# Sums of weights and of operands moved from GpSimd to VectorE, and splits, takes and casts reordered around them, in a two-layer kernel with seven-product blocks

## The reference

```python
# layer 0: grouped convolution along the row, context and bias, then a dense layer with a low-rank part
out = conv(x, weight, groups=4, taps=9) + (cond @ c_weight.T)[:, :, None] + bias[None, :, None]
y   = out @ W.T + b                                   # 1024 -> 1024, on 2048 rows
probs = softmax(out @ gate_w.T + gate_b)              # 4 ranks: 8, 16, 32, 64
r   = the rank with the largest probability
x   = x + y + out @ A[:r].T @ B[:, :r].T

# layer 1: channels mixed by eight kernels weighted per sample, then a dense layer with 8 experts of rank 16
agg = einsum('bk,koi->boi', softmax(mlp(cond)), weight)
out = einsum('boi,bih->boh', agg, x) + agg_b[:, :, None]
w   = sparsemax(out @ W_router.T + b_router)
x   = x + out @ W_base.T + b_base + sum_e w_e (out @ A_e) @ B_e
```

## Time and profile before

| | us |
|---|---|
| median of 3 executions (525.5 to 528.06) | 525.73 |
| the profiled execution | 524.66 |
| its span, first to last instruction | 522.9 |
| TensorE busy with matmuls | 510.3 (98%) |
| VectorE busy | 349.2 (67%) |
| GpSimd busy | 166.5 (32%) |
| ScalarE busy | 129.2 (25%) |

### The profile page before, as it was taken

One profiled execution on the slowest core, in us unless ns is written; L12 is line 12 of the kernel. 1 busy time (PEld: TensorE's weight loads), 2 busy tenths in 40 slices (PEclk: granted clock), 3 DMA queues, 4 the chain that ended last, 5 costly groups with the idle time before them and its releaser, 6 DMA issues.

```text
span 522.9 us, 8726 instructions
## 1 busy us (share of the span) xinstructions
PE 510.3 (98%) x3237; PEld 481.5 (92%) x3237; DVE 349.2 (67%) x743; ACT 129.2 (25%) x270; POOL 166.5 (32%) x142
## 2 busy tenths in 40 slices
PE   8999999989999999999999979999999999999997
PEld 7899999989999999999998869999999999999986
DVE  1865598757666775767787488494867756585752
ACT  3721233313322222331252221111212111111200
POOL 1000771404434042432103353260616235070620
PEclk8999999999999999999999989999999999999999
DMA  8825304427476573656899943332514233340212
GB/s 288 325 76 178 132 2 135 133 67 222 143 249 204 189 261 122 233 159 229 263 418 310 411 149 105 104 123 81 181 52 167 84 116 107 109 155 18 100 46 80
DMA packets 41383, 85.32 MB, mean 163 GB/s; under 512 B 3931, under 2 KB 25435, under 8 KB 41340
## 3 DMA queue, kind: packets, MB, share of 16 engines
q1 hardware_dynamic: 31884, 61.38, 34.8%
q10 hardware_dynamic: 9456, 23.38, 12.3%
HBM read 59.30 MB, written 25.44 MB: 162 GB/s over the span
## 4 chain that ended last, share of the span: by engine, by line
PE 81%; DVE 8%; DMA 7%; issue 2%; SPq 1%; ACT 1%; POOL 0%; DVEq 0%; ACTq 0%
PE b_x L1154 6%; PE b_x L1156 6%; PE b_x L1157 6%; PE b_m L1103 5%; DMA x_scratch<-xs 4%; PE b_p L1138 4%; PE b_y L1154 4%; PE b_p L1140 4%; PE b_p L1139 4%; PE b_y L1157 4%; PE b_y L1156 4%; PE b_m L1115 2%; DMA xs<-x_scratch 2%; PE b_w L1156 2%; PE b_w L1154 2%
## 5 line engine op out<-in xcount | busy, mean ns | idle before, releaser
L489 POOL TENSOR_TENSOR xs<-xs,filt 128x464 f32<-128x464 f32 (+1 forms) x32 | 44.3, 1391 | 127.7 <-DMA xs<-x_scratch 127.6
L542 ACT CAST a_hi<-mixed 128x512 fp32r<-128x512 f32 x64 | 38.7, 619 | 167.5 <-DVE mixed L807 93.7
L819 DVE TENSOR_TENSOR s_lo<-mixed,s_hi 128x512 fp32r<-128x512 f32 x56 | 65.9, 1193 | 18.6 <-ACT s_hi L554 16.3
L1138 PE MATMUL b_p<-wp_hi,a_hi 128*128 128x232 f32 (+1 forms) x224 | 61.5, 275 | 0.5 <-DVE xs L910 0.5
L1139 PE MATMUL b_p<-wp_lo,a_hi 128*128 128x232 f32 (+1 forms) x224 | 61.5, 275 | 0.0
L1140 PE MATMUL b_p<-wp_hi,a_lo 128*128 128x232 f32 (+1 forms) x224 | 61.4, 274 | 0.0
L900 DVE TENSOR_TENSOR xs<-b_x,xs 128x464 f32<-128x464 f32 (+1 forms) x58 | 36.1, 622 | 33.4 <-PE b_x L1157 25.5
L462 POOL TENSOR_TENSOR mixed<-mixed 128x512 f32<-128x512 f32 x14 | 18.1, 1294 | 114.6 <-DVE a_lo L812 97.2
L554 ACT CAST s_hi<-mixed 128x512 fp32r<-128x512 f32 x56 | 34.8, 622 | 75.7 <-POOL mixed L462 35.7
L812 DVE TENSOR_TENSOR a_lo<-mixed,a_hi 128x512 fp32r<-128x512 f32 x64 | 45.2, 728 | 11.2 <-ACT a_hi L542 10.5
L1154 PE MATMUL b_x<-wb_hi,s_hi 128*128 128x464 f32 (+1 forms) x112 | 43.7, 390 | 3.0 <-DVE xs L900 3.0
(11 more groups left out here) (229 smaller groups left out, 1218.9 us busy)
## 6 DMA issues: line engine op xcount, KB each, us to landing
blk<-in_xblk SPq DMA_DIRECT2D x16, 516.0 KB, 3.7
blk<-x_scratch SPq DMA_DIRECT2D x16, 512.0 KB, 3.8
xs<-in_x SPq DMA_DIRECT2D x16, 296.0 KB, 4.7
x_scratch<-xs SPq DMA_DIRECT2D x16, 296.0 KB, 3.5
xs<-x_scratch SPq DMA_DIRECT2D x16, 280.0 KB, 3.2
out_dram<-xs SPq DMA_DIRECT2D x16, 280.0 KB, 2.5
w_raw<-in_wcat SPq DMA_DIRECT2D x8, 546.0 KB, 8.1
praw<-in_wcat ACTq DMA_DIRECT2D x8, 464.0 KB, 4.3
```

Source lines behind the costliest of these rows:

```text
L489: pool.tensor_tensor(xs[s][:, a:b], xs[s][:, a:b], bbase[:, a:b], ALU.add).then_inc(x_biased[q], 1)
L542: act.copy(a_hi[:, op, :, :], mixed[:, op, :, :]).then_inc(ahi_done[op], 1)
L819: dve.tensor_tensor(s_lo[:, i, :, :], mixed[:, S_AT[i], :, :], hi(s_hi[:, i, :, :]), ALU.subtract).then_inc(slo_done[i], 1)
L1138: pe.matmul(dst, x_hi, wp_hi[:, k, 0:PLAIN[l]], start=(k == 0), stop=False)
```

## The change

GpSimd loses the 16 subtractions of the sums of weights and the four operations of `sums(2)`; both become VectorE's (`t_sums(kc)` and `first_sums()`). ScalarE's and VectorE's lists are reordered around them: `split_ut(2)` and `gate_exp(3)` stand at other places, the splits of T3 come before `finish(0, 1)`, released by a new semaphore `b12_read` (after step k = 3 of tile 3) instead of by the end of tile 3. `finish(1, 1)` is taken apart: `take_plain` and the take of `b_z` come ahead of the splits of A21 and A22, the take of `b_w` behind `first_sums()`. In pair 2 VectorE's splits of S1 to S4 come ahead of the first take, and `split_ut(4)` comes behind `sum_mix(6, 0)`; ScalarE's four casts of S come ahead of `gate_exp(4)`. TensorE's and SyncE's lists keep their order; TensorE only signals `b12_read` in addition. The semaphores of the T sums exist for four slots instead of seven.

```diff
@@ GpSimd
-            pool.wait_ge(wlo_done, 2 * NCH)
-            pool.wait_ge(alo_done[A22], 2)
-            for kc in range(HK):
-                pool.tensor_tensor(raw_block(kc, 0), raw_block(kc, 1), raw_block(kc, 0), ALU.subtract).then_inc(t_sum, 1)
...
-            pool.wait_ge(gated, 4 * (2 * FULL + 2))
-            sums(FULL)
@@ ScalarE
             gate_exp(2)
-            split_ut(2)
             for kc in (2, 3):
                 for i in (T1, T2, T4):
                     split_t(i, kc)
-            gate_exp(3)
-            act.wait_ge(dense0_done, 4)
+            split_ut(2)
+            act.wait_ge(b12_read, 1)
             for kc in range(HK):
                 split_t(T3, kc)
+            gate_exp(3)
...
             split_a(A22, 2)
+            for i in S_ORDER:
+                split_s(i, FULL)
@@ VectorE
+            def t_sums(kc):
+                dve.tensor_tensor(raw_block(kc, 0), raw_block(kc, 1), raw_block(kc, 0), ALU.subtract).then_inc(t_sum, 1)
+                dve.tensor_tensor(raw_block(kc, 1), raw_block(kc, 3), raw_block(kc, 1), ALU.subtract).then_inc(t_sum, 1)
+                dve.wait_ge(t_sum, 4 * kc + 1)
+                dve.tensor_tensor(raw_block(kc, 3), raw_block(kc, 3), raw_block(kc, 0), ALU.subtract).then_inc(t_sum, 1)
+                dve.wait_ge(t_sum, 4 * kc + 3)
+                dve.tensor_tensor(raw_block(kc, 2), raw_block(kc, 2), raw_block(kc, 3), ALU.subtract).then_inc(t_sum, 1)
+            def first_sums():
+                dve.tensor_tensor(mixed[:, A22, :, :], mixed[:, A21, :, :], mixed[:, A22, :, :], ALU.add).then_inc(s_sum, 1)
+                dve.tensor_tensor(mixed[:, A21, :, :], mixed[:, A11, :, :], mixed[:, A21, :, :], ALU.subtract).then_inc(s_sum, 1)
+                dve.wait_ge(s_sum, 1)
+                dve.tensor_tensor(mixed[:, A11, :, :], mixed[:, A22, :, :], mixed[:, A11, :, :], ALU.subtract).then_inc(s_sum, 1)
+                dve.wait_ge(s_sum, 3)
+                dve.tensor_tensor(mixed[:, A12, :, :], mixed[:, A12, :, :], mixed[:, A11, :, :], ALU.subtract).then_inc(s_sum, 1)
...
             finish(1, 0)
+            t_sums(0)
+            t_sums(1)
             for i in (T1, T2, T4):
                 split_t(i, 0)
-            gate0(2)
+            t_sums(2)
             for i in (T1, T2, T4):
                 split_t(i, 1)
-            split_ut(2)
+            gate0(2)
+            t_sums(3)
             for kc in (2, 3):
                 for i in (T1, T2, T4):
                     split_t(i, kc)
+            split_ut(2)
+            for kc in range(HK):
+                split_t(T3, kc)
             finish(0, 1)
             gate0(3)
...
             sum_mix(5, 1)
+            take_plain(1, 1)
+            finish_first(1, 1)
             split_a(A21, 2)
             split_a(A22, 2)
-            finish(1, 1)
-            for kc in range(HK):
-                split_t(T3, kc)
+            first_sums()
+            finish_second(1, 1)
...
                 gate(2 * g + 1)
+                if g == FULL:
+                    for i in S_ORDER:
+                        split_s(i, g)
                 if g == PAIRS:
                     split_slot(B21, 1)
                 else:
                     take_first(g)
-                if g == FULL:
-                    split_ut(2 * g)
-                    for i in S_ORDER:
-                        split_s(i, g)
                 if g < LAST:
                     sum_mix(2 * g + 2, 0)
-                if g > FULL:
-                    split_ut(2 * g)
+                split_ut(2 * g)
@@ TensorE, in dense0
+                if T == 2 * FULL - 1 and k == HK - 1:
+                    ins.then_inc(b12_read, 1)
```

More of the change, by code:

```diff
@@ L188, in build @@
         t_sum = sem("t_sum")
-        thi_done = [sem(f"thi_done{i}") for i in range(SLOTS)]
-        tlo_done = [sem(f"tlo_done{i}") for i in range(SLOTS)]
+        thi_done = {i: sem(f"thi_done{i}") for i in SUMS_AT}
+        tlo_done = {i: sem(f"tlo_done{i}") for i in SUMS_AT}
         lbhi_done, lblo_done, bias_split = sem("lbhi_done"), sem("lblo_done"), sem("bias_split")
@@ L204, in build @@
         mix_done, sum_done = sem("mix_done"), sem("sum_done")
-        dense0_done = sem("dense0_done")
+        dense0_done, b12_read = sem("dense0_done"), sem("b12_read")
         pl_done = sem("pl_done")
@@ L967, in _, with finish_first, finish_second, finish @@
             split_ut(0)
-            def finish(s, g):
+            def finish_first(s, g):
                 dve.wait_ge((c11_done, c21_done)[s], g + 1)
                 take((b_x, b_z)[s], 2 * s, g, (fin11, fin21)[s])
+            def finish_second(s, g):
                 dve.wait_ge((c12_done, c22_done)[s], g + 1)
                 take((b_y, b_w)[s], 2 * s + 1, g, (fin12, fin22)[s])
+            def finish(s, g):
+                finish_first(s, g)
+                finish_second(s, g)
                 take_plain(s, g)
```

## The result

| | us | executions |
|---|---|---|
| before, beside the changed kernel | 525.5 (522.83 to 528.06) | 9 |
| the changed kernel | 520.91 (518.71 to 524.89) | 9 |
| ratio | 0.9935, 95% interval 0.9908 to 0.9961 | |
| profiled execution, its span, its clock | 520.59, 518.9, 0.999 | 1 |

The forecast was 523.6, in a range of 522.5 to 525.5: the direction was right, the size was not. The two other batches in which the changed kernel ran gave 0.9946 (0.9922 to 0.9971) and 0.9944 (0.9918 to 0.997), and medians of 523.0 and 522.64, so 520.91 is also a lucky median.

What follows compares the result with a forecast made beforehand. TensorE, busy for 510.3 of 522.9 us, was taken as the bound. Losing waits of 0.48 and 1.57 us takes the profiled 524.66 to 522.6, or 523.7 against the median, stated as 523.6; range 522.5 to 525.5.

Steps and rivals of the forecast that it cites:

- The two waits: TensorE's waits at `plain(5)`, 0.48 us, and at P5 of pair 2, 1.57 us, both forecast to go.
- VectorE's prices: VectorE's new list: 2.2 us per group of weight sums, 2.56 for tile 2's gate, 2.4 for four rests of S.
- Its cover: Margin by which `split_ut(4)` ends before TensorE wants it at `turn_u(5)`: 101.5 against 102.2, so 0.7 us.
- some tenths that TensorE needs to get going: Slow first matmul after a TensorE wait, 0.43 instead of 0.36 us; forecast set at 523.6, not 523.7.
- P5 can follow at 104.85: In pair 2, P4's last matmul starts at 104.5 and P5 follows without a wait: 1.57 us gone.
- what TensorE wants: At `rank0(2)`, TensorE was said to want `split_ut(2)` at 74.91; forecast to end at 74.3.
- faster by over 0.5%: Outcome under 523.1 us for the whole kernel: the second rival and about a fifth of the forecast's cases, chance 0.24.
- The second rival: More than the two waits: part of the 3.0 us layer-turn wait goes or restarts cost more; 522.7 to 523.1, chance 0.12.
- the likeliest case: The forecast itself for the whole kernel, both waits gone: 523.6 us, own range 523.0 to 524.4, chance 0.63.
- The dependent sums and the rule: VectorE's 16 weight sums: 8.8 us forecast, against 9.6 if each cost its full 0.60 by the skill's rule.

Runs made afterwards that it cites:

- experiment 3: Changed kernel with `take_plain` back behind the splits of A21 and A22 and `first_sums()` behind `finish(1, 1)`'s last part: 522.59 us, 0.995 to the kernel before.
- experiment 4: Changed kernel with `split_ut(4)` moved one step back, behind `sum_mix(6, 1)`: 523.97 us, 0.9975 to the kernel before.
- experiment 6: Changed kernel with the four sums of operands of pair 2 back on GpSimd, behind its memset: 524.48 us, 0.9984 to the kernel before.
- experiment 5: Changed kernel with the 16 sums of weights back on GpSimd, other steps in the changed order: 526.32 us, 1.0017 to the kernel before.
- experiment 7: Changed kernel with 24 unneeded additions on GpSimd beside VectorE's sums of weights: 531.48 us in one execution.
- experiment 10: Changed kernel with the first 432 columns of two of four `xs` regions for pair 8 loaded earlier: 523.86 us, 0.9959 to the kernel before.

## Why the prediction missed, step by step

**What held.** The two waits went, both and fully. VectorE's prices came out as worked out: 2.19 to 2.20 us per group of sums (2.2 forecast), 2.57 for the gate (2.56), 2.48 for the rests of S (2.4), 2.54 for the four sums of operands (2.5). From there the whole list was right to some tenths, in its own time (the start is 1.11 later, by `turn_u(2)`): T3's rests, the takes, `gate0(3)` waiting for TensorE's `b_p`. `split_ut(4)` ended at 102.60 - 1.11 = 101.49, where 101.5 was forecast. Its cover was 0.34 us instead of 0.7 because TensorE came at 102.94 - 1.11 = 101.83 and not at 102.2: the mistake of the next paragraph, seen from the other side.

**The term that was mis-sized** is the worth of the two waits: "So the change can give back at most about 0.48 + 1.57 = 2.05 us". That took the bracket for the price. The bracket counts from the end of the last matmul's row, but in a full pipeline the next one starts long before that end: rows of 0.36 us start 0.20 apart. By starts, from these rows of the kernel before and those of the earlier trace rows:

```profile
74.69 0.35 PE L1227 MATMUL b_w<-wb_hi,a_lo 128*128 128x432 f32 x1
75.21 0.36 PE L1184 MATMUL b_x<-lb_lo,ut_lo 97*128 97x432 f32 x1
...
89.89 0.27 PE L1140 MATMUL b_p<-wp_hi,a_lo 128*128 128x228 f32 x1
90.86 0.28 PE L1139 MATMUL b_p<-wp_lo,a_hi 128*128 128x228 f32 x1
...
107.17 0.36 PE L1156 MATMUL b_y<-wb_lo,s_hi 128*128 128x432 f32 x1
```

| | last start to first start | ordinary pitch | next pitch, ordinary | worth | bracket |
|---|---|---|---|---|---|
| `plain(5)` | 90.65 - 89.89 = 0.76 | 0.11 | 0.21, 0.11 | 0.75 | 0.48 |
| P5 of pair 2 | 106.90 - 104.96 = 1.94 | 0.20 | 0.27, 0.20 | 1.81 | 1.57 |

The landmarks say 0.74 and 1.81, and experiments 3, 4 and 6 put waits back and found the same 0.25 us on top. Two things make it up: the distance from start to start holds 0.17 us more than the bracket, and the step behind it is slow by 0.07 to 0.10. The prediction did have the second, "some tenths that TensorE needs to get going", and counted it the right way, 523.7 down to 523.6; it left out the first. In the same way "P5 can follow at 104.85" counted to the end of the last matmul (104.5 + 0.36); its pitch gives 104.7.

**A third wait that no view listed.** `turn_u(2)` to `(3)` is 0.13 to 0.15 us shorter. Before, `split_ut(2)` ended at 74.85 and `rank0(2)` started at 74.91, 0.22 us behind the last matmul (row of 74.69) instead of 0.19, and the next step took 0.30 (row of 75.21) instead of 0.20: released, not ready. A gap of that size stands in no bracket. These rows account for the 0.13; no run isolates it. The prediction read 74.91 as what TensorE wants; it was what TensorE got.

Together 0.74 + 1.81 + 0.13 = 2.68 instead of the 2.05 forecast, which is 0.51% of 525.5. The right term would have given 525.73 - 2.7 = 523.0, and by my estimate would have put the chance of "faster by over 0.5%" at about one half instead of 0.24. It would not have saved the range.

**The range** is the second step that failed: it had no term for the scatter of the turn and the start-up. From 523.0 to 520.91 it is another 2.1 us, which didn't come back: the same kernel had medians of 523.0 and 522.64 in other batches. Which stage gave them in the nine executions of the first batch stays open, since only one of them was profiled. I gave the likeliest case a width of 1.4 us for a median of a few executions, though the profile before already showed a second stage, the turn, with a wait of 3.0 us on loads. Over the executions profiled here that stage takes 61.8 to 68.2 us, the start-up 37.8 to 40.9. The second rival came closest in number (522.7 to 523.1 for "more than the two waits") and gave two reasons, the turn and the restart. The restart was right. The turn was not: it took 66.60, 66.75 before and 64.36, 67.19, 67.67 after.

**The clock at the turn.** One part of its scatter is TensorE's granted clock. The changed kernel's second and third executions, slices of 4 us with the granted clock behind the five busy times:

```profile
292.00:296.00 4.00, 1.06 (x9) 0.87 (x8) 0.21 (x1) 0.00 (x0) 1.16 (x1) 0.90 1.02 422
296.00:300.00 4.00, 3.51 (x9) 3.07 (x10) 1.48 (x3) 0.00 (x0) 2.54 (x2) 0.50 0.63 252
300.00:304.00 4.00, 4.00 (x20) 3.65 (x20) 3.92 (x6) 0.62 (x1) 1.32 (x2) 0.75 0.34 114
```

```profile
292.00:296.00 4.00, 1.13 (x11) 0.94 (x10) 0.64 (x1) 0.00 (x0) 1.16 (x1) 1.00 1.02 423
296.00:300.00 4.00, 3.08 (x14) 2.46 (x15) 1.28 (x3) 0.00 (x0) 2.88 (x3) 1.00 0.52 208
300.00:304.00 4.00, 2.56 (x18) 2.30 (x17) 4.00 (x5) 0.62 (x1) 0.99 (x1) 1.00 0.48 144
```

In the first of these the clock goes to 0.50, which is 1.2 GHz, around a wait of 3.43 us, and TensorE does 9 matmuls where the other does 14. In the second, with waits of 2.87, 0.92 and 1.44 us, it stays at 2.4 GHz; the turn takes about the same in both. What decides between the two isn't settled by these runs.

**The dependent sums and the rule.** Rows of the changed kernel: 59.73 to 60.25, 0.52 between two sums that don't wait for each other, though each is busy for 0.60; 60.76 to 61.40, 0.64 before the one that does wait. The Trainium skill, "VectorE: DVE Perf Modes", section "The DRAIN you can't avoid", has the next operation start only when the pipeline is empty, and says that leaving out semaphores doesn't help; but it adds that an operation which isn't held starts earlier, which the prediction left out. The trace agrees with the addition and not with the part on semaphores: without one the next sum starts 0.08 us before the row's end, with one 0.04 after it. By the rule without its addition the 16 sums would take 9.6 us; the trace has 8.8.

## What to carry to other kernels

Price a wait of TensorE from start to start: the distance between the last matmul before it and the first behind it, less the ordinary pitch, plus the slow second step. At full clock that was some 0.25 us more per wait than the idle time shown; and look at the granted clock behind the wait, for where it fell (experiments 5 and 7) a single wait cost another 1.6 to 1.7 us. Ask of a cover, too, when TensorE will come once its waits are gone. Moving elementwise work off GpSimd can be free even on an engine that is busier in the profile, because what GpSimd does beside VectorE can lengthen VectorE's own instructions; ask for both halves at once, since one alone may bring nothing. And compare kernels by landmarks inside one stretch: here they gave the effect to 0.01 us where medians of 9 to 12 executions left it within 0.25%; a wait that is missing is a gain only if the landmarks behind it have come earlier too.

## What the runs showed of the hardware

- 128x256 additions of GpSimd on unrelated memory make VectorE's instructions with two operands in SBUF 1.01 us instead of 0.60 (128x432), three rests 2.89 instead of 1.64, and a scan of 128x4 0.39 instead of 0.17 (experiment 7). A memset of 128x2048 on GpSimd, 1.82 us long, did not: four rests beside it took 2.16 us in the changed kernel, where four took 2.15 with GpSimd idle.
- The granted clock fell to about half at the turn around waits of 2.34 to 4.07 us in seven profiles (2.34, 2.59, 2.83, 2.97, 3.41, 3.43, 4.07), and in the stretch of the change behind 3.49 and 3.80 us in experiments 5 and 7. No fall stands at a shorter wait. The clock stayed at 1.00 around one of 2.87 us at the turn, around 3.08 at `turn_u(2)` in experiment 7 and around 3.44 in pair 7 of experiment 10: the length of the wait alone doesn't tell.
- Behind the waits of experiments 5 and 7 the clock was low for some 3 to 4 us, and that cost 1.6 to 1.7 us.
- TensorE's matmuls of 432 columns start 0.20 us apart at full clock, in rows of 0.36 us, and up to 0.39 apart at about half clock, behind the wait of experiment 5.
